# Decoder layer on one core: causal masks in VectorE's maxima, one transpose for a pair's maxima, results by ScalarE and GpSimd

## The chip, the cores and the metric

One Trainium2 chip, one NeuronCore of it. The metric is the device time of one launch in microseconds (us): 2375.72 us, the median of 3 runs (2371.66 to 2376.65). PE is TensorE's matmul side and PEld its weight load, DVE is VectorE, ACT is ScalarE, POOL is GpSimd, SP is SyncE.

## What is computed

A decoder layer for 8 sequences of 512 rows and 256 columns: linear attention, then the block that the change touches, then eight experts. The touched block is self attention with a causal mask plus cross attention to 1024 context rows, 16 heads of 16 columns each:

```python
att = jnp.where(causal[None, None], jnp.einsum('bhqd,bhkd->bhqk', q, k) * scale, -jnp.inf)
y = jnp.einsum('bhqk,bhkd->bhqd', jax.nn.softmax(att, axis=-1), v)
attc = jnp.einsum('bhqd,bhkd->bhqk', qc, kc) * scale
y = y + jnp.einsum('bhqk,bhkd->bhqd', jax.nn.softmax(attc, axis=-1), vc)
return y.transpose(0, 2, 1, 3).reshape(x.shape[0], T, C) @ Wp + bp
```

## The kernel before

The eight sequences are eight passes of one loop, each written out by hand for every engine. The part of a pass that the change touches treats the 16 heads as 8 pairs (`PAIRS`); the two heads of a pair stand on partitions 0 to 63 and 64 to 127 of `hq` (queries) and `hk` (keys), 16 columns split into high and low parts. Each pair goes through four kinds of work.

**Maxima.** The softmax needs each query row's largest score. A pair has 22 units (`MAXES`), 11 for each head. `max_unit` (L684) multiplies 128 queries with up to 512 keys into one of three PSUM banks, and `reduce` (L1297) takes the maximum over the columns into `craw`. 16 units are cross scores (L702, reduced at L1308, 512 columns each). The last 6 are self scores (L696, reduced at L1305): widths 512, then 384 and 128 together, then 256, each for both heads, so 8 matmuls and 8 reductions. The causal mask of their last 128 columns is added by TensorE itself, two bf16 matmuls of 128 columns for each (L698, `iden2` times `mqk2`, high and low rows of the partition half).

**The row.** After the last unit VectorE puts the maxima into `mpad` with two small operations (L1316, L1317). TensorE turns `mpad` with four 128 x 128 transposes (`maxima_rows`, L711), one for each block of 128 queries, and ScalarE copies the bank to `mrow` in one piece (L1112). Rows of `mrow`, times -1 in `minus`, are later subtracted from the scores by matmuls (L733, L739).

**Weights.** A pair has 11 units (`NU`): 3 of self and 8 of cross scores. `exp_scores` computes the transposed scores and subtracts the maxima in PSUM (`eslot`, two of them), ScalarE takes the exponential (L1118) into `es` (four of them, `ERING`), POOL zeroes what lies above the diagonal in the self units (L612), and `weigh` (L767) multiplies with the values, whose 17th column is 1 and gives the sum of the weights.

**Results.** After a pair's last `weigh`, ScalarE copies the sums to `zk` (L1127), `turn_results` (L771) transposes them into the next free one of the same three banks (L778), and VectorE's `results` (L1319) takes the reciprocals of the weight sums (L1324), multiplies (L1325), and adds self and cross parts into `y_s` (L1329). It waits for each step by a semaphore.

The order of all this is one list, `ORDER`, that `heads_order` writes and that every engine follows. In a repeated group of two weight units stand: two maxima units, the turn of an earlier pair if one is due, two `weigh`, two maxima units, two `exp_scores`. The maxima units belong to the pair after the one whose weights are taken (`AHEAD`), and the row follows four units after its last maximum (`ROW_AFTER`), for the last pair at once. The maxima, rows and turns share the ring of three banks: entry n may be written when entry n - 3 has been read (`ring_slot`, L673), and what reads it is VectorE for a maximum and a turn, ScalarE for a row:

```python
                    if kind == "row":
                        pe.wait_ge(s_mrow, cur(b, PAIRS, p + 1))
                    else:
                        pe.wait_ge(s_red, cur(b, NRED, RED_AT[former]))
```

Pair 0's maxima run before this, between feature products of the next pass (`FIRST_PARTS`); pairs 1 to 7 have theirs beside the weights of pairs 0 to 6; pair 7's weights have no maxima beside them. As a pair has 11 weight units and a group two, the turn falls alternately ahead of a pair's first self maxima and between the first and second two of them.

Of the kernel before, what the change touches and what calls it, by code (L numbers as in the profile page):

```python
# [21 lines left out]
P = 128  # L22
# [16 lines left out]
NEG = -1e30  # L39
HROW = 4 * XD  # L40
ZW = 32
# [56 lines left out]
BEHIND = 4  # L98

# [61 lines left out]

RING = [e for e in ORDER if e[0] in ("max", "row", "turn")]
RING_AT = {e: n for n, e in enumerate(RING)}
NRING, NRED = len(RING), sum(e[0] != "row" for e in RING)
RED_AT = {e: sum(f[0] != "row" for f in RING[:n + 1]) for n, e in enumerate(RING)}
# [39 lines left out]
def attentions(nc, x, xT, ctxT, wqkT, wv_l, rf, w_out, b_out, wk, bk, wq, bq, wv, bv, wck, bck,  # L205
# [9 lines left out]
    with ctx:  # L215
# [11 lines left out]
        mpad = sb("mpad", [P, NT, P])  # L227
# [19 lines left out]
        iden2 = sb("iden2", [P, 2, P], BF16)  # L247
        mqk2 = sb("mqk2", [P, 2, P], BF16)
# [40 lines left out]
        cstage = r_s[:, 0:3, :].rearrange("p n (s c) -> p n s c", s=2)  # L289
# [9 lines left out]
        minus = sb("minus", [P, 2], F32R)  # L299
        zk = sb("zk", [P, 2, T // 2])  # L300
# [76 lines left out]
        s_keep = sem("s_keep")  # L377
        s_ys = sem("s_ys")
        s_pace = sem("s_pace")
        s_blank = sem("s_blank")  # L380
        s_sent = sem("s_sent")
        s_route = sem("s_route")
        s_eid = sem("s_eid")

# [6 lines left out]
        LOADS = 42  # L391
# [7 lines left out]
        def _(sp):  # L399
# [29 lines left out]
            for n, src in enumerate((ident_d, mask_qk, mask_kq)):  # L429
                for half in range(2):  # L430
                    for at in range(2):
                        const(cstage[at * HROW:(at + 1) * HROW, n, half, :], src[half * HROW:(half + 1) * HROW])
# [120 lines left out]
            sp.wait_ge(s_av, NEXP * (nb + 1))  # L553
            for e in range(E):
                sp.dma_start(w2s[:, e * NHC * C:(e + 1) * NHC * C].rearrange("p (k c) -> p k c", k=NHC),
                             w2T[e].rearrange("(k p) c -> p k c", p=P)).then_inc(s_w2, 16)
# [9 lines left out]
        def _(pool):  # L566
# [14 lines left out]
            with pool.Fori(0, nb) as b:  # L581
# [23 lines left out]
                for p in range(PAIRS):  # L605
                    for n in range(NSELF):
                        k = p * NU + n
                        pool.wait_ge(s_exp, cur(b, NEXP, k + 1))
                        pool.sem_inc(s_past, 1)
                        for j, col in EXP_SELF[n]:  # L610
                            block = es[:, k % ERING, :].rearrange("p (a c) -> p a c", a=HB)[:, :, col:col + P]
                            last = nc.gpsimd.affine_select(block, block, [[0, HB], [1, P]], ALU.is_ge, 0.0, base=0,  # L612
                                                           channel_multiplier=-1)
                        last.then_inc(s_cut, 1)
# [13 lines left out]
        def _(pe):  # L628
# [44 lines left out]
            def ring_slot(b, entry):  # L673

                n = RING_AT[entry]
                if n >= MBANKS:
                    kind, p, _ = former = RING[n - MBANKS]
                    if kind == "row":
                        pe.wait_ge(s_mrow, cur(b, PAIRS, p + 1))
                    else:  # L680
                        pe.wait_ge(s_red, cur(b, NRED, RED_AT[former]))
                return mbank[n % MBANKS]

            def max_unit(b, p, m):  # L684
# [8 lines left out]
                if n >= 2 * NT:  # L693
                    for t, col in MAX_SELF[n - 2 * NT]:
                        w = (t + 1) * P
                        mm(pb[:, col:col + w], hq[i][at, t * P:(t + 1) * P], hk[i][at, 0:w], start=True, stop=False)  # L696
                        for half in range(2):
                            last = mm(pb[:, col + w - P:col + w], iden2[at, half, :], mqk2[at, half, :],  # L698
                                      start=False, stop=half == 1)
# [6 lines left out]
            def maxima_rows(b, p):  # L706
# [328 lines left out]
        def _(act):  # L1035
            act.sem_inc(s_mrow, PAIRS)
            act.sem_inc(s_exp, NEXP)
            act.sem_inc(s_keep, PAIRS)

# [11 lines left out]
            with act.Fori(0, nb) as b:  # L1051
# [54 lines left out]
                def maxima_rows(p):  # L1106
# [5 lines left out]
                    nc.scalar.activation(mrow[p % 2][:], mbank[n % MBANKS], ACT.Copy).then_inc(s_mrow, 1)  # L1112
# [15 lines left out]

                for kind, p, n in ORDER:
                    if kind == "row":  # L1130
                        maxima_rows(p)
# [582 lines left out]
```

## Time and profile before

| | us |
|---|---|
| median of 3 runs | 2375.72 |
| profiled execution, its own time | 2378.1 |
| its span | 2376.3 |
| PE busy | 2275.0 |
| DVE busy | 1400.3 |
| ACT busy | 1048.2 |
| POOL busy | 309.8 |

The busy time of a matmul reaches from its start to a modelled end, and neighbours overlap, so a share near 100% doesn't say that PE could take no more. In the timelines each line is one or several like instructions in a row; the bracket gives how long the engine stood idle before, and what ended that.

### The profile page before, as it was taken

The numbers are of one execution on the slowest core, as the hardware profiler recorded it, in microseconds if no ns is written. First come the engines' busy times: TensorE is split into PE (matmuls) and PEld (weight loads), VectorE is DVE, ScalarE is ACT, GpSimd is POOL, SyncE is SP. The second block draws the span as 40 slices with busy tenths as digits, with TensorE's granted clock in tenths as the row PEclk, the third lists the DMA queues.
The fourth block names the chain that finished last, engine by engine and source line by source line (L and its number), as shares of the span: only waits on it lengthen the run. The fifth ranks groups of instructions, "written<-read, shape, count | busy, mean of one in ns | idle before, by whom it ended". The sixth has DMA issues, their size and how long they took to land. (4 is left out here: it accounts for less than half of the span.)

```text
span 2376.3 us, 52163 instructions
## 1 busy us (share of the span) xinstructions
PE 2275.0 (96%) x17506; PEld 1439.5 (61%) x17507; DVE 1400.3 (59%) x3568; ACT 1048.2 (44%) x1432; POOL 309.8 (13%) x516
## 2 busy tenths in 40 slices
PE   8999999999999999999999999999999999799998
PEld 4556565656465556555565656564655565399997
DVE  2488347844685458734883478446854587244554
ACT  1256524652366226632564246513662266333332
POOL 1100011001110111011001111011101110122222
PEclk9989998999899989999899989998999999899999
DMA  7530034102520162006200441025201620555553
GB/s 231 202 105 24 2 131 163 46 2 81 191 68 2 47 225 68 2 11 226 81 24 2 150 144 46 2 81 191 68 2 43 229 68 2 179 182 179 178 185 113
DMA packets 115433, 236.19 MB, mean 99 GB/s; under 512 B 18638, under 2 KB 42319, under 8 KB 113008
## 3 DMA queue, kind: packets, MB, share of 16 engines
q1 hardware_dynamic: 111776, 224.55, 27.8%
q0 software_dynamic: 3408, 8.41, 1.0%
q8 instruction: 145, 2.38, 0.4%
q14 instruction: 104, 0.85, 0.1%
HBM read 160.66 MB, written 73.17 MB: 98 GB/s over the span
## 5 line engine op out<-in xcount | busy, mean ns | idle before, releaser
L1118 ACT ACTIVATE es<-ps 128x1024 f32<-128x1024 f32 (+1 forms) x704 | 659.9, 983 | 336.8 <-PE ps L739 252.6
L1308 DVE TENSOR_REDUCE craw<-ps 128x1 f32<-128x512 f32 x1024 | 641.1, 684 | 192.2 <-PE ps L702 180.5
L702 PE MATMUL ps<-hk,hq 64*128 64x512 f32 x1024 | 302.0, 497 | 20.0 <-DMA hq<-scr_qc 15.0
L767 PE MATMUL ps<-es,vca 128*17 128x256 f32 x4096 | 276.7, 382 | 1.2
L702 PEld LDWEIGHTS ps<-hk,hq 64*128 64x128 f32 x1024 | 143.1, 197 | 189.2 <-DVE craw L1308 109.8
L1305 DVE TENSOR_REDUCE craw<-ps 128x1 f32<-128x512 f32 (+3 forms) x512 | 218.7, 484 | 53.6 <-PE ps L698 49.8
L737 PE MATMUL ps<-hq,hk 64*128 64x512 f32 x1024 | 238.1, 429 | 1.5 <-ACT es L1118 1.5
L612 POOL TENSOR_SCALAR_AFFINE_SELECT es<-es 128x256 f32<-128x256 f32 x256 | 99.4, 407 | 1045.9 <-ACT es L1118 1045.9
L739 PE MATMUL ps<-mrow,minus 64*128 64x512 f32 x1024 | 219.1, 394 | 0.0
L1619 ACT ACTIVATE hT<-ph,b1s 128x128 f32<-128x128 f32 x312 | 89.2, 369 | 183.9 <-PE ph L1582 183.9
L767 PEld LDWEIGHTS ps<-es,vca 128*17 128x17 f32 x4096 | 93.8, 96 | 115.0 <-issue 62.4
L1582 PEld LDWEIGHTS ph<-xinT,w1s 128*128 128x128 f32 x1248 | 148.3, 195 | 3.1 <-issue 1.1
L1582 PE MATMUL ph<-xinT,w1s 128*128 128x128 f32 x1248 | 148.6, 278 | 0.7 <-ACT xinT L1609 0.7
L1595 PE MATMUL py<-w2s,hT 128*128 x624 | 141.1, 379 | 0.0
L787 PE MATMUL ps<-xT_s,wqf 128*128 128x512 f32 x288 | 138.5, 607 | 1.6 <-DVE wkf L1187 1.6
L737 PEld LDWEIGHTS ps<-hq,hk 64*128 64x128 f32 x1024 | 110.7, 186 | 40.8 <-ACT es L1118 23.3
L696 PE MATMUL ps<-hk,hq 64*128 64x512 f32 (+3 forms) x512 | 130.0, 388 | 4.6 <-DVE craw L1308 3.4
L797 PE MATMUL ps<-wkf,xT_s 128*128 128x512 f32 x288 | 130.3, 597 | 0.0
L1595 PEld LDWEIGHTS py<-w2s,hT 128*128 128x128 f32 x624 | 115.5, 190 | 14.1
L739 PEld LDWEIGHTS ps<-mrow,minus 64*128 64x128 f32 x1024 | 116.0, 187 | 9.9
L824 PE MATMUL ps<-big_b,x_s 128*128 128x512 f32 x256 | 118.2, 615 | 0.9 <-DVEq L1213 0.7
L1324 DVE RECIPROCAL rec<-ps 128x16 f32<-128x16 f32 x64 | 16.0, 250 | 172.1 <-PE ps L778 172.1
(206 smaller groups left out, 2883.6 us busy)
## 6 DMA issues: line engine op xcount, KB each, us to landing
w1s<-in_w1T SPq DMA_DIRECT2D x39, 1024.0 KB, 5.4
hk<-scr_kc SPq DMA_DIRECT2D x64, 512.0 KB, 5.4
scr_kc<-staged SPq DMA_DIRECT2D x16, 1024.0 KB, 4.7
scr_qc<-staged SPq DMA_DIRECT2D x32, 512.0 KB, 4.9
scr_q<-staged SPq DMA_DIRECT2D x32, 512.0 KB, 5.5
hq<-scr_qc SPq DMA_DIRECT2D x64, 256.0 KB, 5.0
hq<-scr_q SPq DMA_DIRECT2D x64, 256.0 KB, 4.2
hk<-scr_k SPq DMA_DIRECT2D x64, 256.0 KB, 5.1
```

Source lines behind the costliest of these rows:

```text
L696: mm(pb[:, col:col + w], hq[i][at, t * P:(t + 1) * P], hk[i][at, 0:w], start=True, stop=False)
L702: last = mm(pb, hq[i][at, T + t * P:T + (t + 1) * P], hk[i][at, T + half * BANK:T + (half + 1) * BANK], start=True, stop=True)
L737: mm(pb[a], hk[i][at, T + j * P:T + (j + 1) * P], hq[i][at, T:2 * T], start=True, stop=False)
L739: last = mm(pb[a], neg[a], mrow[p % 2][at, :], start=False, stop=True)
L767: last = mm(z[row:row + VW, (2 - len(tiles)) * P:2 * P], (va if own else vca)[:, j, p * HB + a, :], weights, start=n in (0, NSELF), stop=n ...
L787: last = mm(t[:, a * T:(a + 1) * T], wqf[:, c, j * P:(j + 1) * P], xT_s[:, c, :], start=c == 0, stop=c == KC - 1)
L797: last = mm(t[:, half * 512:(half + 1) * 512], xT_s[:, c, i * P:(i + 1) * P], wkf[:, c, half * 512:(half + 1) * 512], start=c == 0, stop=c ...
L1118: nc.scalar.activation(es[:, k % ERING, :].rearrange("p (a c) -> p a c", a=HB)[:, :, 0:w], eslot[k % 2][:].rearrange("p (a c) -> p a c", a ...
L1305: last = v.reduce_max(craw[p % 2][:, t, a:a + 1, 2], pb[:, col:col + (t + 1) * P], AX.X)
L1308: last = v.reduce_max(craw[p % 2][:, t, a:a + 1, half], pb, AX.X)
L1582: last = mm(ph[g % 2][:, a * TILE:(a + 1) * TILE], w1s[i][:, k, (GROUP * c + a) * P:(GROUP * c + a + 1) * P], xinT[i][:, k, :], start=k == ...
L1595: last = mm(py[i][:, n, 0:C], hT[i][:, c, n * P:(n + 1) * P], w2s[:, bass.ds(e * (NHC * C) + c * C, C)], start=c == 0, stop=c == NHC - 1)
```

## The change

- The self maxima lose their mask matmuls (L698). VectorE adds the mask instead: one `tensor_tensor_reduce` reads the scores in PSUM, adds `causal` (bf16, 384 zeros and then the triangle of mask values, of which the last columns are taken), writes the sum back over the scores and gives the maximum.
- The maxima of all four query blocks go into one 128 x 128 `mpad`, 16 columns for each head and block, by one operation. One transpose turns it. ScalarE fills `mrow` with four copies of the same 128 columns, each scaled for each partition by `inblock` (1 where the partition belongs to that block, else 0). `minus` has -1 in the two rows of each block.
- A turned result is copied by ScalarE to `zt` in SBUF (`turned`), VectorE takes only the reciprocals from it, and POOL multiplies and adds. This holds for pairs 0 to 6; the last pair stays with VectorE. VectorE's reciprocals stand two maxima units later in its own order (`DVE_ORDER`, `LATER`). The bank of a turn is free when ScalarE has copied it.
- At the start, 11 small loads of constants are gone and the masks' tiles are built otherwise. `sp` waits once more before the loads of the experts' weights.

```diff
@@ order and ring @@
+def reciprocals_later():
+    order = [e for e in ORDER if e[0] in ("max", "turn")]
+    for p in range(PAIRS - 1):
+        at = order.index(("turn", p, 0))
+        order.insert(min(at + 1 + LATER, order.index(("turn", p + 1, 0))), order[at])
+        del order[at]
+    return order
...
                     if kind == "row":
                         pe.wait_ge(s_mrow, cur(b, PAIRS, p + 1))
+                    elif kind == "turn" and former != LAST_TURN:
+                        pe.wait_ge(s_zt, cur(b, PAIRS - 1, p + 1))
                     else:
                         pe.wait_ge(s_red, cur(b, NRED, RED_AT[former]))
@@ TensorE @@
                     for t, col in MAX_SELF[n - 2 * NT]:
                         w = (t + 1) * P
-                        mm(pb[:, col:col + w], hq[i][at, t * P:(t + 1) * P], hk[i][at, 0:w], start=True, stop=False)
-                        for half in range(2):
-                            last = mm(pb[:, col + w - P:col + w], iden2[at, half, :], mqk2[at, half, :],
-                                      start=False, stop=half == 1)
+                        last = mm(pb[:, col:col + w], hq[i][at, t * P:(t + 1) * P], hk[i][at, 0:w], start=True, stop=True)
...
-                for t in range(NT):
-                    last = tr(pb[:, t * P:(t + 1) * P], mpad[:, t, :], ident[:])
-                last.then_inc(s_ring, 1)
+                tr(pb[:, 0:P], mpad[:], ident[:]).then_inc(s_ring, 1)
@@ ScalarE @@
-                    nc.scalar.activation(mrow[p % 2][:], mbank[n % MBANKS], ACT.Copy).then_inc(s_mrow, 1)
+                    for t in range(NT):
+                        last = nc.scalar.activation(mrow[p % 2][:, t * P:(t + 1) * P], mbank[n % MBANKS][:, 0:P],
+                                                    ACT.Copy, scale=inblock[:, t:t + 1])
+                    last.then_inc(s_mrow, 1)
...
+                def turned(p):
+                    s = RING_AT["turn", p, 0]
+                    act.wait_ge(s_ring, cur(b, NRING, s + 1))
+                    act.wait_ge(s_ys, cur(b, PAIRS, p))
+                    tv = mbank[s % MBANKS].rearrange("p (n d) -> p n d", d=ZW)
+                    nc.scalar.activation(zt[:], tv[:, :, 0:VW], ACT.Copy).then_inc(s_zt, 1)
@@ GpSimd @@
+                def results(p):
+                    pool.wait_ge(s_rec, b * (PAIRS - 1) + (p + 1))
+                    pool.sem_inc(s_past, 1)
+                    nc.gpsimd.tensor_tensor(yn[:], zt[:, :, 0:XD], rec[:].unsqueeze(2).broadcast_to([P, 2 * NT * HB, XD]),
+                                            ALU.mult).then_inc(s_yn, 1)
+                    pool.wait_ge(s_yn, b * (PAIRS - 1) + (p + 1))
+                    pool.sem_inc(s_past, 1)
+                    rows = sums_of()
+                    nc.gpsimd.tensor_tensor(y_s[:, :, p * HB * XD:(p + 1) * HB * XD], rows[:, 0], rows[:, 1],
+                                            ALU.add).then_inc(s_ys, 1)
@@ VectorE @@
                     if n >= 2 * NT:
+                        dve.sem_inc(s_held, 1)
                         for t, col in MAX_SELF[n - 2 * NT]:
-                            last = v.reduce_max(craw[p % 2][:, t, a:a + 1, 2], pb[:, col:col + (t + 1) * P], AX.X)
+                            own = pb[:, col:col + (t + 1) * P]
+                            last = v.tensor_tensor_reduce(own, own, causal[:, (NT - 1 - t) * P:NT * P], 1.0, LOWEST,
+                                                          ALU.add, ALU.max, craw[p % 2][:, t, a:a + 1, 0])
...
-                        raw = [craw[p % 2][:, :, :, w] for w in range(3)]
-                        rows = mpad[:].rearrange("p t (a c) -> p t a c", a=HB)
-                        v.tensor_copy(rows[:, :, :, 0], raw[2])
-                        v.tensor_tensor(rows[:, :, :, 1], raw[0], raw[1], ALU.max).then_inc(s_max, 1)
+                        rows = mpad[:].rearrange("p (a t c) -> p t a c", a=HB, t=NT)
+                        v.tensor_tensor(rows[:, :, :, 0:2], craw[p % 2][:, :, :, 0:2], craw[p % 2][:, :, :, 0:3:2],
+                                        ALU.max).then_inc(s_max, 1)
...
+                def reciprocals(p):
+                    dve.wait_ge(s_zt, cur(b, PAIRS - 1, p + 1))
+                    v.reciprocal(rec[:], zt[:, :, XD]).then_inc(s_rec, 1)
```

VectorE, at the turn that falls ahead of a pair's self maxima, before (from the last cross maximum of the pair to the end of the results; REGISTER_ALU rows are waits):

```order
L1308 TENSOR_REDUCE craw<-ps 128x1
L1322 REGISTER_ALU
L1324 RECIPROCAL rec<-ps 128x16
L1228 REGISTER_ALU
L1325 TENSOR_TENSOR yn<-ps,rec 128x256
L1327 REGISTER_ALU
L1329 TENSOR_TENSOR y_s<-yn 128x4x32
```

and the same place with the change:

```order
L1365 TENSOR_REDUCE craw<-ps 128x1
L1355 REGISTER_ALU
L1361 ISA ps,craw<-ps,causal 128x512
L1361 ISA craw 128x1
L1355 REGISTER_ALU
L1361 ISA ps,craw<-ps,causal 128x512
L1361 ISA craw 128x1
L1377 REGISTER_ALU
L1378 RECIPROCAL rec<-zt 128x16
L1355 REGISTER_ALU
L1361 ISA ps,craw<-ps,causal 128x384
L1361 ISA craw 128x1
```

Two of VectorE's three operations on the results are gone, and the third stands between the self maxima. Each masked maximum is two instructions, the second of which writes `craw` alone.

ScalarE, from the copy of a turned result to the copy of the next pair's maxima, with the change:

```order
L1177 ISA
L1179 ACTIVATE zt<-ps 128x272
L1160 REGISTER_ALU
L1162 ACTIVATE es<-ps 128x1024
L1160 REGISTER_ALU
L1162 ACTIVATE es<-ps 128x1024
L1160 REGISTER_ALU
L1162 ACTIVATE es<-ps 128x1024
L1160 REGISTER_ALU
L1162 ACTIVATE es<-ps 128x1024
L1150 REGISTER_ALU
L1154 ACTIVATE mrow<-ps,inblock 128x128 x4
```

The copy to `zt` (L1179) is new and stands behind the two exponentials of its group; the copies to `mrow` were one of 128 x 512.

## Rows read from the trace of the kernel before

**Rows 1.** The page, part 1: busy time of TensorE, its share of the span, instructions.
```profile
PE 2275.0 (96%) x17506; PEld 1439.5 (61%) x17507; DVE 1400.3 (59%) x3568; ACT 1048.2 (44%) x1432; POOL 309.8 (13%) x516
```
**Rows 2.** Window of two pairs: length, then PE, PEld, DVE, ACT, POOL busy, clock, DMA share.
```profile
441.80:475.90 34.10, 33.79 (x377) 20.65 (x374) 28.85 (x59) 22.67 (x27) 2.79 (x8) 1.00 0.03 11
```
**Rows 3.** Timeline, one steady group: start, length, engine, line, operation, [idle before].
```profile
167.65 1.06 PE L767 MATMUL ps<-es,vca 128*17 128x256 f32 x16
...
169.17 3.98 DVE L1308 TENSOR_REDUCE craw<-ps 128x1 f32<-128x512 f32 x6 [0.21 <-PE ps L702]
...
170.34 1.06 PE L767 MATMUL ps<-es,vca 128*17 128x256 f32 x16
```
**Rows 4.** Timeline, a pair whose turn falls ahead of its self maxima.
```profile
173.21 0.66 PE L778 MATMUL ps<-ident,zk 128*128 128x128 f32 x4
...
175.00 0.51 PE L696 MATMUL ps<-hk,hq 64*128 64x512 f32 x2
...
175.67 1.29 DVE L1305 TENSOR_REDUCE craw<-ps 128x1 f32<-128x512 f32 x2 [0.36 <-PE ps L698]
...
176.45 0.33 PE L696 MATMUL ps<-hk,hq 64*128 64x384 f32 x1
...
177.44 0.41 PE L767 MATMUL ps<-es,va 128*17 128x128 f32 x8
...
178.76 0.76 DVE L1305 TENSOR_REDUCE craw<-ps 128x1 f32<-128x256 f32 x2 [0.16 <-PE ps L698]
...
179.98 2.72 DVE L1308 TENSOR_REDUCE craw<-ps 128x1 f32<-128x512 f32 x4
...
181.40 0.65 PE L711 MATMUL ps<-ident,mpad 128*128 128x128 f32 x4
...
181.98 0.50 PE L737 MATMUL ps<-hq,hk 64*128 64x512 f32 x2
182.09 0.60 ACT L1112 ACTIVATE mrow<-ps 128x512 fp32r<-128x512 f32 x1 [0.85 <-PE ps L711]
```
**Rows 5.** Timeline, a pair whose turn falls between its self maxima.
```profile
157.62 1.29 DVE L1305 TENSOR_REDUCE craw<-ps 128x1 f32<-128x512 f32 x2 [0.84 <-PE ps L698]
...
159.10 0.44 PE L696 MATMUL ps<-hk,hq 64*128 64x384 f32 x1
...
159.97 2.12 DVE L1305 TENSOR_REDUCE craw<-ps 128x1 f32<-128x384 f32 x6
...
162.42 0.50 PE L702 MATMUL ps<-hk,hq 64*128 64x512 f32 x2
...
162.95 2.48 DVE L1308 TENSOR_REDUCE craw<-ps 128x1 f32<-128x512 f32 x4 [0.49 <-PE ps L702]
...
163.68 0.51 PE L702 MATMUL ps<-hk,hq 64*128 64x512 f32 x2
```
**Rows 6.** Timeline of the start: first use of the loaded constants by VectorE and TensorE.
```profile
38.51 0.30 DVE L1191 CAST iden<-r_s 128x256 bf16<-128x256 f32 x1 [20.65 <-DMA gb_bc<-in_gate_b]
...
45.54 1.03 PE L813 MATMUL ps<-wp_s,bv_c 128*128 128x256 f32 x4
```
**Rows 7.** Timeline: pair 0's eight self reductions at a stretch.
```profile
377.23 3.27 DVE L1305 TENSOR_REDUCE craw<-ps 128x1 f32<-128x512 f32 x8
```
**Rows 8.** VectorE: a sum from PSUM by group, and two small operations of the timeline.
```profile
L1272 DVE TENSOR_TENSOR r_s<-ps,xb 128x512 f32<-128x512 f32 x32 | 22.1, 692 | 145.6 <-PE ps L912 103.6 <-PE ps L965 41.9
...
280.87 0.17 DVE L1406 TENSOR_SCALAR mv<-mv 128x4 f32<-128x4 f32 x1
280.94 0.16 DVE L1407 TENSOR_SCALAR mv<-mv 128x4 f32<-128x4 f32 x1
```
**Rows 9.** Groups of the page: a ScalarE operation with a per-partition operand.
```profile
L1619 ACT ACTIVATE hT<-ph,b1s 128x128 f32<-128x128 f32 x312 | 89.2, 369 | 183.9 <-PE ph L1582 183.9
```
**Rows 10.** POOL: a product-sized sum by group, and the wait before a pair's cuts.
```profile
L1523 POOL TENSOR_TENSOR base<-xin,b2s 128x256 f32<-128x256 f32 x39 | 28.8, 740 | 14.4 <-issue 13.6
...
187.44 0.41 POOL L612 TENSOR_SCALAR_AFFINE_SELECT es<-es 128x256 f32<-128x256 f32 x1 [14.16 <-ACT es L1118]
```

More of the change, by code:

```diff
@@ L39 @@
 NEG = -1e30
+LOWEST = -3.0e38
 HROW = 4 * XD
+MROW = HROW // NT
 ZW = 32
@@ L98 @@
 BEHIND = 4
+LATER = 2
 SWAP = (0, 1)
@@ L160 @@
 ORDER = heads_order()
+def reciprocals_later():
[5 more added lines that the diff above has]
+    return order
+DVE_ORDER = reciprocals_later()
 RING = [e for e in ORDER if e[0] in ("max", "row", "turn")]
 RING_AT = {e: n for n, e in enumerate(RING)}
-NRING, NRED = len(RING), sum(e[0] != "row" for e in RING)
-RED_AT = {e: sum(f[0] != "row" for f in RING[:n + 1]) for n, e in enumerate(RING)}
+NRING, NRED = len(RING), sum(e[0] == "max" for e in RING) + 1
+LAST_TURN = ("turn", PAIRS - 1, 0)
+RED_AT = {e: sum(f[0] == "max" or f == LAST_TURN for f in RING[:n + 1]) for n, e in enumerate(RING)}
 NEXP = PAIRS * NU
@@ L226, in attentions @@
         mrow = [sb(f"mrow{i}", [P, T], F32R) for i in range(2)]
-        mpad = sb("mpad", [P, NT, P])
+        mpad = sb("mpad", [P, P])
+        zt = sb("zt", [P, 2 * NT * HB, VW])
+        sb("spare", [P, (NT - 1) * P - 2 * NT * HB * VW])
         wq_s = sb("wq_s", [P, KC, C])
@@ L390, in attentions @@
         WJ = NPAIR // 2
-        LOADS = 42
+        LOADS = 31
         SEL_DMA = 4 * NQ
@@ L428, in _ @@
             const(number[:], number_d)
-            for n, src in enumerate((ident_d, mask_qk, mask_kq)):
-                for half in range(2):
-                    for at in range(2):
-                        const(cstage[at * HROW:(at + 1) * HROW, n, half, :], src[half * HROW:(half + 1) * HROW])
+            const(r_s[:, 0, 0:P], mask_qk)
             const(wvl[:], wv_l.rearrange("(k p) r -> p k r", p=P))
@@ L1131, in _ @@
                         maxima_rows(p)
+                    elif kind == "turn" and p < PAIRS - 1:
+                        turned(p)
                     elif kind == "exp":
@@ L1197, in _ @@
                             iota[:, 0:E].unsqueeze(1).broadcast_to([P, E + 1, E]), ALU.is_gt)
-            for a in range(HB):
-                at = slice(a * HROW, (a + 1) * HROW)
-                v.tensor_scalar(minus[at], ident[at, a * HROW:a * HROW + 2], -1.0, None, ALU.mult)
+            v.reduce_sum(minus_f[:], ident[:].rearrange("p (b c) -> p c b", c=MROW)[:, 0:2, :], AX.X)
+            v.reduce_sum(inblock[:], ident[:].rearrange("p (a t c) -> p t a c", a=HB, t=NT), AX.XY)
             v.tensor_tensor(bv_c[:, 0, :], bv_c[:, 0, :], bv_c[:, 1, :], ALU.add).then_inc(s_fold, 1)
@@ L1327, in results @@
                     dve.wait_ge(s_red, cur(b, NRED, RED_AT["turn", p, 0]))
-                    rows = yn[:].rearrange("p (w t a) d -> p w t (a d)", w=2, t=NT)
+                    rows = sums_of()
                     v.tensor_tensor(y_s[:, :, p * HB * XD:(p + 1) * HB * XD], rows[:, 0], rows[:, 1], ALU.add).then_inc(s_ys, 1)
                     dve.wait_ge(s_ys, cur(b, PAIRS, p + 1))
-                for kind, p, n in ORDER:
+                for kind, p, n in DVE_ORDER:
                     if kind == "max":
                         reduce(p, n)
+                    elif kind == "turn" and p == PAIRS - 1:
+                        last_results()
                     elif kind == "turn":
-                        results(p)
+                        reciprocals(p)
                 dve.wait_ge(s_xb, cur(b, 2, 2))
```

52 lines of the change are left out of this document (33 added, 19 removed).

## The prediction

> **What bounds the kernel now.** I read the page first. TensorE is busy 96% of the span and VectorE 59% [rows 1], which would make this a TensorE kernel in which VectorE costs nothing. But the average covers three different stages, and a matmul's busy time reaches to a modelled end. So I went on to a window of two pairs inside the touched stage: 34.10 us, or 17.05 us a pair, of which VectorE is busy 28.85 us, 85% [rows 2]. ScalarE has 22.67 us and POOL 2.79 us. Both TensorE and VectorE are near their limit there, and which one waits has to be read from the timeline.
>
> In a steady group TensorE's `weigh` returns every 2.69 us (167.65 to 170.34), while VectorE stands idle 0.21 us before it goes on [rows 3]. TensorE sets the pace and VectorE follows with a tenth to spare. Around the self maxima this differs from pair to pair. With the turn ahead of them, TensorE issues the turn at 173.21 and the first self maximum only at 175.00. VectorE fills that hole with the results and is still idle 0.36 us before it reduces at 175.67 [rows 4]. With the turn between them, the results stand in VectorE's way: the next self maximum is issued at 159.10, its reduction starts at 159.97 [rows 5].
>
> **The change, part by part.** In a pass 7 pairs have their maxima beside weights. I count 3 with the turn ahead, 3 with it between, and 1 without a turn.
>
> *TensorE, masks.* From the first self maxima to the next maxima it takes 175.00 to 176.45, 1.45 us [rows 4]; the same step with unmasked maxima takes 162.42 to 163.68, 1.26 us [rows 5]. So four mask matmuls cost 0.19 us, and a pair's sixteen 0.76 us.
>
> *TensorE, the row.* Four transposes hold it from 181.40 to 181.98, 0.58 us [rows 4]; three fewer save 0.43 us. Together TensorE sheds 1.19 us a pair, and no pair can gain more.
>
> *VectorE, masked maxima.* The eight self reductions of a pair take 3.27 us in a row [rows 7]. Each becomes a sum with a maximum plus a second instruction that writes the maximum. Let x be what one costs above the reduction it replaces. No row shows the new operation, so I bound it. A sum of 512 columns from PSUM takes 0.692 us [rows 8]; two reductions of that size take 1.29 us together [rows 4], 0.645 each with their overlap. So the sum itself adds 0 to 0.05. The second instruction is small: two small operations without a wait between them start 0.07 us apart (280.87, 280.94), and one lasts 0.17 us [rows 8]. That gives x = 0.07 at the least and 0.22 if nothing overlaps. I don't exclude less than 0.07 by rows, but a second instruction can't be free. I take 0.11, nearer the lower end: the pair has no semaphore between its halves.
>
> The Trainium skill ("VectorE: DVE Perf Modes", section "Two Vector instructions with no wait between them") says that an operation which also writes out its accumulator is two instructions, and that the second is judged on its own for being held. By that the read-out would not be held here, all operands starting at partition 0, and the sum would go by the lower end. No run here shows it.
>
> *VectorE, results and row.* The product and the sum leave; the reciprocals stay at no more than 0.25 us, and as they now read SBUF I take 0.20. Of the two operations for `mpad` one goes, 0.08 us: the step from the last reduction's end (178.76 + 0.76 = 179.52) to the next (179.98) shrinks from 0.46 to 0.38 [rows 4].
>
> *Turn ahead.* From first self reduction to first cross reduction it is now 179.98 - 175.67 = 4.31 us [rows 4]. After: it begins 0.19 earlier (no masks) and lasts 3.27 + 8x + 0.20 + 0.38. VectorE reaches the next pair 0.65 - 8x earlier. The results that left had been in a hole, and the reciprocals move from the hole into the busy stretch. The row's transposes wait for the maxima that VectorE takes next, and with their 0.43 TensorE gains 1.08 - 8x.
>
> *Turn between.* Now 162.95 - 157.62 = 5.33 us [rows 5]. The maximum at 159.10 comes 0.19 earlier, its reduction can start 0.48 behind it (175.67 - 175.00 less 0.19), at 159.39. Then 2.12 + 6x + 0.20 + 0.38 reaches 162.09 + 6x instead of 162.95. With the row: 1.29 - 6x.
>
> *No turn.* As the first, without reciprocals: 1.28 - 8x.
>
> *ScalarE.* `mrow` takes four operations with a per-partition operand; such ones take 89.2 / 312 = 0.286 us each [rows 9], so 1.14 us instead of 0.60. ScalarE stood idle 0.85 us before it [rows 4] and the row comes earlier, so most is covered; between 0 and the full 0.54 I take 0.1, since the exponentials behind it have two buffers. The copy to `zt` is shorter than 0.60 us and finds an engine that is a third idle [rows 2]. Behind it stand the next exponentials; if they come late, TensorE's `exp_scores` is next to wait.
>
> *POOL.* Two operations of at most 0.74 us each [rows 10], while the next pair's cuts are awaited for 14.16 us. They cost nothing; without this cover they would delay the cuts, and `weigh` behind them, by 1.5 us a pair. They release `zt` long before the next turn.
>
> *Pair 0.* There the eight reductions stand in a row [rows 7] and TensorE waits. They get 8x - 0.08 longer, and TensorE gets 0.43 back: a loss of 8x - 0.51.
>
> *The start.* VectorE has the constants at 38.51 and TensorE needs them at 45.54 [rows 6]. Eleven loads fewer make them earlier, which nobody waits for. Semaphore bookkeeping and the last pair are costed at nothing; their work lies behind TensorE's features.
>
> *Sum per pass:* 3 (1.08 - 8x) + 3 (1.29 - 6x) + (1.28 - 8x) - 0.7 for ScalarE - (8x - 0.51) = 8.20 - 58x us. With x = 0.11 that is 1.82 us, times 8 passes 15 us. The profiled execution's own time is 2378.1 us, 2.4 above the median, so it would give 2363, and the median goes from 2375.7 to **2361 us**. The sum is zero at x = 0.141. With x = 0.07 it is 33 us, 2343; with 0.22 it is -36 us, 2412.
>
> **Rivals.**
>
> *VectorE becomes the bound, slower.* Place: the self maxima of every pair. If the second instruction runs without overlap (x = 0.20), the loss is 3.4 us a pass, 27 us in all: 2403. It decides from x = 0.141. For it: VectorE is at 85% already, and in the stretch with the turn ahead it loses its hole. Against: small operations without waits do overlap. Chance 0.25.
>
> *The masked maximum runs at half rate.* It reads a bank and writes the same one. Each of the eight would last another 3.27 / 8 = 0.41 us, x = 0.52: 8.20 - 30.2 = -22.0 us a pass, 2552. The sum from PSUM at 0.692 speaks against it. The Trainium skill ("Vector Engine (DVE) Microarchitecture Reference", section "Points that are easy to get wrong") has a rule near it, that an accumulating operation of the scalar-tensor-tensor shape runs at half throughput with two non-bf16 sources in SBUF; here one source is in PSUM and the other bf16, so its condition isn't met. Chance 0.05.
>
> *Nothing measurable.* x between 0.131 and 0.151 leaves less than 5 us, the 0.2% that a measurement of this kernel can tell from no change: 2376. Chance 0.13.
>
> *TensorE gains all it sheds.* 1.19 us for 7 pairs and 8 passes is 67 us: 2309. It needs x near 0, against the second instruction that the program shows. Chance 0.05; the forecast has 0.52.
>
> **The numbers.** Faster by over 0.2%: forecast and full gain, 0.57. Within: 0.13. Slower: 0.30. The range reaches down to x = 0.07 with ScalarE costing nothing (8.20 + 0.7 - 4.06 = 4.84 us a pass, 39 us: 2337) and up to x = 0.20, 2403.
>
> **What would show it.** Right: the masks' matmuls gone, the `weigh` period of 2.69 us unchanged, a self stretch (first masked maximum to first cross reduction) of 4.7 us with the turn ahead, eight masked maxima some 0.9 us above 3.27, VectorE's idle time before the self maxima about 1 us with the turn ahead, a pair near 16.8 us instead of 17.05. Wrong: second instructions 0.15 us apart or more from the next, TensorE waiting for the masked maxima between self units, or exponentials starting late behind `mrow`.

## The result and the profile after

| | before | after |
|---|---|---|
| median, us | 2374.26 (4 runs) | 2342.89 (4 runs) |
| profiled execution: span, us | 2376.3 | 2340.5 |

The ratio is 0.9863, 95% interval 0.9843 to 0.9884: 28 to 37 us faster, 31 by the medians and 35.8 by the two spans. Forecast were 15 us and 2361; the direction was right, the size half of what came.

Part 1 of the page of the kernel after, beside [rows 1]:

```profile
PE 2231.4 (95%) x16290; PEld 1402.7 (60%) x16291; DVE 1369.7 (59%) x3905; ACT 1098.8 (47%) x1680; POOL 368.3 (16%) x628
```

TensorE has 1216 instructions fewer: 1024 mask matmuls and 192 transposes. VectorE is busy 31 us less although it has 337 instructions more, 512 of them read-outs. The groups of the new operations (us busy, mean ns of one | us idle before, and what ended that):

```profile
L1361 DVE CUSTOM_DVE_ANT_0 ps<-ps,causal 128x512 f32<-128x512 f32 (+3 forms) x512 | 235.5, 517 | 78.8 <-PE ps L741 78.8
L1154 ACT ACTIVATE mrow<-ps,inblock 128x128 fp32r<-128x128 f32 x256 | 73.4, 375 | 80.5 <-PE ps L752 80.5
L645 POOL TENSOR_TENSOR yn<-zt,rec 128x256 f32<-128x256 f32 x56 | 34.9, 622 | 253.8 <-DVE rec L1378 253.8
L650 POOL TENSOR_TENSOR y_s<-yn 128x128 f32<-128x128 f32 x56 | 25.7, 459 | 10.0 <-POOL yn L645 10.0
L1179 ACT ACTIVATE zt<-ps 128x272 f32<-128x272 f32 x56 | 22.2, 397 | 8.6 <-PE ps L818 8.6
L1378 DVE RECIPROCAL rec<-zt 128x16 f32<-128x16 f32 x56 | 13.9, 248 | 104.3 <-ACT zt L1179 104.3
```

The timeline after, of a pair whose turn falls ahead of its self maxima, as [rows 4]:

```profile
171.56 0.66 PE L818 MATMUL ps<-ident,zk 128*128 128x128 f32 x4
...
173.36 0.50 PE L741 MATMUL ps<-hk,hq 64*128 64x512 f32 x2
...
174.04 0.70 DVE L1361 CUSTOM_DVE_ANT_0 ps<-ps,causal 128x512 f32<-128x512 f32 x1 [1.34 <-PE ps L741]
...
174.66 0.14 DVE L1361 DVE_READ_ACCUMULATOR2_ANT craw<- 128x1 f32 x1
174.66 0.73 DVE L1361 CUSTOM_DVE_ANT_0 ps<-ps,causal 128x512 f32<-128x512 f32 x1
...
178.08 2.68 DVE L1365 TENSOR_REDUCE craw<-ps 128x1 f32<-128x512 f32 x4
...
179.50 0.32 PE L752 MATMUL ps<-ident,mpad 128*128 128x128 f32 x1
...
179.86 1.14 ACT L1154 ACTIVATE mrow<-ps,inblock 128x128 fp32r<-128x128 f32 x4 [0.67 <-PE ps L752]
...
181.24 1.06 PE L807 MATMUL ps<-es,vca 128*17 128x256 f32 x16
```

From the first self reduction to the first cross reduction it is now 178.08 - 174.04 = 4.04 us, where it was 4.31. The prediction had named 4.7 us for this stretch as a sign of being right, and about 1 us for VectorE's idle time ahead of it, which is 1.34. The line to look at is the read-out, the second instruction of a masked maximum: it starts at 174.66, the very moment at which the next masked maximum starts. From one masked maximum of 512 columns to the next it is 0.62 us.

The same for a pair whose turn falls between its self maxima, as [rows 5], down to the same `weigh` four pairs later:

```profile
155.62 0.63 PE L807 MATMUL ps<-es,va 128*17 128x256 f32 x8
...
158.19 0.58 PE L741 MATMUL ps<-hk,hq 64*128 64x384 f32 x3
...
158.88 0.57 DVE L1361 CUSTOM_DVE_ANT_0 ps<-ps,causal 128x384 f32<-128x384 f32 x1 [0.61 <-PE ps L741]
...
161.65 2.48 DVE L1365 TENSOR_REDUCE craw<-ps 128x1 f32<-128x512 f32 x4
...
163.06 0.32 PE L752 MATMUL ps<-ident,mpad 128*128 128x128 f32 x1 [0.17 <-DVE craw L1365]
...
221.84 0.63 PE L807 MATMUL ps<-es,va 128*17 128x256 f32 x8
```

and of the kernel before, the same stretch with its results, its transposes and the `weigh` behind them:

```profile
156.40 0.63 PE L767 MATMUL ps<-es,va 128*17 128x256 f32 x8
...
159.56 0.29 DVE L1329 TENSOR_TENSOR y_s<-yn 128x128 f32<-128x128 f32 x1
...
164.37 0.65 PE L711 MATMUL ps<-ident,mpad 128*128 128x128 f32 x4 [0.18 <-DVE craw L1308]
164.95 1.06 PE L767 MATMUL ps<-es,vca 128*17 128x256 f32 x16
...
225.28 0.63 PE L767 MATMUL ps<-es,va 128*17 128x256 f32 x8
```

From the first `weigh` row to the last, four pairs, it is 68.88 us before and 66.22 after. This **four-pair period** is free of the start, the end and the noise of whole runs (the second pass gives 68.87 and 66.24), so it is taken from every kernel below. Counted from one pair later it is 68.87 and 66.23; where a kernel's period depends on the pair from which it is counted, that is said.

### The profile page after: what moved, and what is told of

Same layout as the page of the kernel before. It is cut to its first block and busy times, and to the rows that moved or that the text cites. A ratio compares the mean times of both kernels' runs of the same rounds, so it can differ in the third digit from the quotient of the medians.

```text
span 2340.5 us, 50923 instructions
## 1 busy us (share of the span) xinstructions
PE 2231.4 (95%) x16290; PEld 1402.7 (60%) x16291; DVE 1369.7 (59%) x3905; ACT 1098.8 (47%) x1680; POOL 368.3 (16%) x628
## 5 line engine op out<-in xcount | busy, mean ns | idle before, releaser
L744 PE MATMUL ps<-hk,hq 64*128 64x512 f32 x1024 | 310.1, 503 | 20.2 <-DMA hq<-scr_qc 14.8
L1361 DVE CUSTOM_DVE_ANT_0 ps<-ps,causal 128x512 f32<-128x512 f32 (+3 forms) x512 | 235.5, 517 | 78.8 <-PE ps L741 78.8
L744 PEld LDWEIGHTS ps<-hk,hq 64*128 64x128 f32 x1024 | 153.5, 197 | 190.4 <-DVE craw L1365 118.7
L741 PE MATMUL ps<-hk,hq 64*128 64x512 f32 (+3 forms) x512 | 124.6, 373 | 10.1 <-DVE craw L1361 5.1
L952 PE MATMUL ps<-big_c,big_a 128*128 128x256 f32 x512 | 112.6, 381 | 2.8 <-ACT big_c L1122 2.8
```

The source lines that it names most:

```text
L741: last = mm(pb[:, col:col + w], hq[i][at, t * P:(t + 1) * P], hk[i][at, 0:w], start=True, stop=True)
L744: last = mm(pb, hq[i][at, T + t * P:T + (t + 1) * P], hk[i][at, T + half * BANK:T + (half + 1) * BANK], start=True, stop=True)
L1361: last = v.tensor_tensor_reduce(own, own, causal[:, (NT - 1 - t) * P:NT * P], 1.0, LOWEST, ALU.add, ALU.max, craw[p % 2][:, t, a:a + 1, 0])
```

## Experiments

Three readings stood against each other: two engines share the bound, by the forecast's formula (A); TensorE alone bounds (B); VectorE alone bounds (C). Each run undoes a part of the change, or does one alone. The cuts of code show the lines that matter most.

**Masks by TensorE again**, with VectorE's plain maxima, the rest as changed:

```diff
-                        last = mm(pb[:, col:col + w], hq[i][at, t * P:(t + 1) * P], hk[i][at, 0:w], start=True, stop=True)
+                        mm(pb[:, col:col + w], hq[i][at, t * P:(t + 1) * P], hk[i][at, 0:w], start=True, stop=False)
+                        for half in range(2):
+                            last = mm(pb[:, col + w - P:col + w], iden2[at, half, :], mqk2[at, half, :],
+                                      start=False, stop=half == 1)
```

> The changed kernel with the masks back on TensorE (two bf16 matmuls each, as before) and plain maxima on VectorE; the single transpose and the results' new owners stay. Changed kernel: 2343 us. Theory A (the two engines share the bound: what TensorE sheds in masks VectorE gets in return, 0.76 us against 0.4 us a pair, and half the stretches are limited by each): some 1 us a pass is lost, about 2350. Theory B (TensorE alone is the bound): all 0.76 us of 8 pairs and 8 passes are lost, 49 us, about 2392. Theory C (VectorE alone is the bound): 0.4 us a pair is won, 24 us, about 2319.

Measured: 2355.06 us, ratio 0.9911 (0.9888 to 0.9934), period 67.93. Slower by 12 us, where A said some 7, B 49, and C said faster: nearest to A. The masks gain where they are, on VectorE.

**Four transposes again**, of the one `mpad`, with the four scaled copies kept:

```diff
-                tr(pb[:, 0:P], mpad[:], ident[:]).then_inc(s_ring, 1)
+                for t in range(NT):
+                    last = tr(pb[:, t * P:(t + 1) * P], mpad[:], ident[:])
+                last.then_inc(s_ring, 1)
```

> The changed kernel, but the one transpose of the row is issued four times, to the four quarters of the bank (only the first is read). This adds TensorE's 0.43 us a pair and nothing else. Theory A and theory B: 0.43 us for 8 pairs and 8 passes, 27 us slower, about 2370. Theory C: the row's transposes lie beside VectorE's work, no more than 5 us slower.

Measured: 2363.53, ratio 0.9948 (0.9933 to 0.9963), period 67.30. 20.6 us slower, where A and B said 27 and C at most 5. The three transposes are worth 1.08 us in four pairs, less than the 1.72 (4 times 0.43) forecast.

**Results by VectorE again**, at the old place in its order:

```diff
-                    elif kind == "turn" and p == PAIRS - 1:
-                        last_results()
                     elif kind == "turn":
-                        reciprocals(p)
+                        last_results(p)
```

> The changed kernel with the results as before: VectorE takes reciprocals, product and sum from the bank right at the turn, ScalarE and POOL have no part in them. Theory A: VectorE has a hole where the turn falls ahead of the self maxima, and is in the way only where it falls between them: 0.8 us lost in 3 pairs, 0.16 us won in 3, 1.9 us a pass, 15 us slower, about 2358. Theory C: 0.87 us in 6 pairs and 8 passes, 42 us slower, about 2385. Theory B: the same as the changed kernel, 2343.

Measured: 2356.5, ratio 0.9921 (0.9898 to 0.9944), period 67.55, or 67.18 counted from one pair later. By the time this is A's 2358; what the loss is made of is another matter (below, at the masks alone).

**Maxima without the mask.** Plain reductions over the same columns, masked ones included; so the mask is left out of the maxima, and the weights above the diagonal are still zeroed by POOL:

```diff
-                            last = v.tensor_tensor_reduce(own, own, causal[:, (NT - 1 - t) * P:NT * P], 1.0, LOWEST,
-                                                          ALU.add, ALU.max, craw[p % 2][:, t, a:a + 1, 0])
+                            last = v.reduce_max(craw[p % 2][:, t, a:a + 1, 0], pb[:, col:col + (t + 1) * P], AX.X)
```

> The changed kernel with plain maxima over the unmasked self scores: the mask is left out of the maxima (not out of the weights, where GpSimd's cuts stay), so a row subtracts a larger number than it needs, which cancels in the softmax. It takes the masked maximum's extra cost x away and gives x by the trace. Theory A: 0.38 us of VectorE a pair are on the path wherever it is late: 2.6 us a pass, 21 us faster, about 2322. Theory B: no change, 2343. Theory C: 24 us faster, about 2319.

Measured: 2327.12, ratio 0.9795 (0.9773 to 0.9818), period 64.91, which beats both kernels. It lies nearer to A (2322) and C (2319) than to B (2343); C was excluded by the first run. A maximum over more columns is still an upper bound, and the softmax divides it out again, as long as no masked score stands so far above a row's others that their exponentials vanish. Its timeline at the place of 174.04 above:

```profile
173.89 0.50 PE L741 MATMUL ps<-hk,hq 64*128 64x512 f32 x2
...
174.43 1.29 DVE L1359 TENSOR_REDUCE craw<-ps 128x1 f32<-128x512 f32 x2 [1.19 <-PE ps L741]
...
175.79 2.01 DVE L1359 TENSOR_REDUCE craw<-ps 128x1 f32<-128x384 f32 x6
...
178.07 1.29 DVE L1362 TENSOR_REDUCE craw<-ps 128x1 f32<-128x512 f32 x2
```

This prices the operation directly: 178.07 - 174.43 = 3.64 us against 4.04, so 0.40 for eight, **x = 0.05 us**. The periods say the same: 66.22 - 64.91 = 1.31 for 32, 0.04 each.

The rows show a second price that x doesn't hold. A plain maximum starts 0.54 us after its scores are issued (173.89 to 174.43), a masked one 0.68 (173.36 to 174.04), and the first pass has 0.53 to 0.54 and 0.68 to 0.69 wherever VectorE waits for self scores. Whether the operation makes these 0.14 or the semaphore increment that stands ahead of it (`s_held`, gone in this run too) was not tried.

Beside the first run this one prices the mask matmuls alone, as VectorE works alike in both: 67.93 - 64.91 = 3.02 us for 64, **0.76 us a pair**, all of what the forecast said TensorE would shed. The masked maxima take 1.31 of it back, and 1.71 is left, 0.43 a pair.

**The reciprocals at once** (`LATER = 0` instead of 2), with the masked and with the unmasked maxima:

> The changed kernel with LATER = 0: VectorE takes the reciprocals right behind the turn in its order instead of two maxima units later. Changed kernel: 2343. Theory A: 0.16 us of reciprocals leave the busy stretch for the hole ahead of or between the self maxima, in 6 pairs of 8 passes, 8 us, about 2335. The rival: ScalarE's copy to zt comes too late behind its exponentials, VectorE waits for it, and the maxima behind it with it; 0.3 us in 6 pairs would be 14 us slower, about 2357.

> The unmasked maxima (the mask left out of the maxima alone, as in the run before) with LATER = 0. Unmasked alone: 2327. Theory A: another 8 us, about 2319. If TensorE is the bound once VectorE has the masks off: 2327.

Measured: 2339.85, ratio 0.9842 (0.9818 to 0.9866), period 66.08; and 2326.23, ratio 0.9776 (0.9751 to 0.9801). The intervals overlap those of the kernels with 2. A's 8 us aren't seen in either, nor the rival's loss; the second came out at the 2327 expected if TensorE bounds once the masks are off VectorE. The periods of the second are 64.72 and, counted from one pair later, 64.68 where it was 64.90; of the first, 66.08 and 66.46, 0.14 less and 0.23 more. So where the reciprocals stand is worth some 0.2 us in four pairs, with the masked maxima in either direction; it isn't settled whether anything in the whole run.

**One part alone, with the row half undone.** Masks alone, then results alone, each with four transposes and the four scaled copies (the edits are those above, combined):

> Of the change only the masks in VectorE's maxima: the results are VectorE's as before, and the row has four transposes (ScalarE's four copies stay). Kernel before: 2376. Theory A with x = 0.05: with the turn ahead of the self maxima the results lie in a hole and 0.37 us is won; with the turn between them the results stay in the way and 0.1 is won; less 0.4 for pair 0: 1.4 us a pass, 11 us, about 2365. Theory B: 0.76 us for 8 pairs and 8 passes, 49 us, about 2327. Theory C: VectorE has 0.4 us more a pair, 24 us slower, about 2400.

> Of the change only the results' new owners (ScalarE copies, VectorE takes reciprocals two units later, POOL multiplies and adds): masks on TensorE as before, four transposes (ScalarE's four copies and the single operation for mpad stay). Kernel before: 2376. Theory A: with masks on TensorE the hole is there in any case; 0.27 less 0.16 us is won in 3 pairs, 3 us, about 2372. Theory C: 0.87 us in 6 pairs and 8 passes, 42 us, about 2334. Theory B: 2376.

Measured: 2372.84, ratio 0.9978 (0.9966 to 0.9991), period 68.62; and 2381.16, ratio 1.0014 (1.0005 to 1.0024), period 69.04. All three readings miss: A by 8 and 9 us, B by 46 and 5, C by 27 and 47. Either ScalarE's copies cost what the parts gain, or the parts gain next to nothing alone. The last four runs separate these. "Old row" is the row as before, save that one operation still fills `mpad`:

```diff
-        mpad = sb("mpad", [P, P])
+        mpad = sb("mpad", [P, NT, P])
...
-                tr(pb[:, 0:P], mpad[:], ident[:]).then_inc(s_ring, 1)
+                for t in range(NT):
+                    last = tr(pb[:, t * P:(t + 1) * P], mpad[:, t, :], ident[:])
+                last.then_inc(s_ring, 1)
...
-                    for t in range(NT):
-                        last = nc.scalar.activation(mrow[p % 2][:, t * P:(t + 1) * P], mbank[n % MBANKS][:, 0:P],
-                                                    ACT.Copy, scale=inblock[:, t:t + 1])
-                    last.then_inc(s_mrow, 1)
+                    nc.scalar.activation(mrow[p % 2][:], mbank[n % MBANKS], ACT.Copy).then_inc(s_mrow, 1)
```

> The kernel before (masks by TensorE, results by VectorE) with the new row alone: one mpad, one transpose, four scaled copies. Additive: the row was worth 20.6 us between the full change and the one with four transposes, 26.3 us between masks on TensorE with and without it; so 2377 less 20 to 26, about 2354, two thirds of the whole gain by itself. Interplay (the row needs VectorE's lighter load to pay): under 12 us, 2366 or more.

> Masks by VectorE alone, with the row as before throughout: four blocks of mpad, four transposes, one copy of 512 columns by ScalarE. Beside the run with four transposes and four copies (2372.8) this takes only ScalarE's three extra copies away. If the copies cost what the forecast gave them, 0.7 us a pass: 2367. If they are hidden: 2373. If they cost their full 0.54 us for each of 7 pairs, 30 us: 2343.

> Results by ScalarE and GpSimd alone, with the row as before throughout. Beside the run with four transposes and four copies (2381.2) this takes only the three extra copies away. Copies at 0.7 us a pass: 2375.5, nothing gained by the results themselves. Copies hidden: 2381. Moving the results pays by itself (VectorE alone bounds): under 2370.

> The whole change except the row: masks by VectorE, results moved, but four blocks of mpad, four transposes and one copy. Beside the run with four transposes and four copies (2363.5): copies at 0.7 us a pass give 2358, hidden copies 2363. With this and the first run of this job the row as a whole (fewer transposes, more copies) is priced on both backgrounds: additive if before less the row alone and this less the whole change are the same within 4 us, about 18 us by the first price.

Measured: 2355.27, 2373.74, 2375.32 and 2361.56 us, before 2375.14 on the same chip. The row is additive, as expected: before less the row alone is 19.9 us, the change with the old row less the whole change 18.7 (these two on different chips). Of the copies, the masks' run says hidden, the results' run says 0.7 us a pass, the last lies between; the periods decide it (below).

All the combinations of the three parts (the ratios are each to the runs of before on its own chip):

| masks by VectorE | results moved | new row | median, us | ratio (95%) | four-pair period, us |
|---|---|---|---|---|---|
| | | | 2374.26 | 1 | 68.88 |
| yes | | | 2373.74 | 0.9998 (0.9984 to 1.0012) | 68.60 |
| | yes | | 2375.32 | 0.9995 (0.9979 to 1.0011) | 69.03 |
| | | yes | 2355.27 | 0.9916 (0.9892 to 0.9941) | 67.96 |
| yes | yes | | 2361.56 | 0.9933 (0.9907 to 0.9958) | 67.29 |
| | yes | yes | 2355.06 | 0.9911 (0.9888 to 0.9934) | 67.93 |
| yes | | yes | 2356.50 | 0.9921 (0.9898 to 0.9944) | 67.55 |
| yes | yes | yes | 2342.89 | 0.9863 (0.9843 to 0.9884) | 66.22 |

By the periods the masks alone gain 0.28 us in four pairs and the results alone lose 0.15. Counted from one pair later the masks alone gain more, 68.87 - 68.23 = 0.64: wherever the masked maxima stand with VectorE's own results 0.37 us are lost at one place in a pass, which is read below. The runs' ratios, 0.9978 and 0.9998 for the masks, 1.0014 and 0.9995 for the results, are a few us either way. Both together gain 1.59 (1.56 from one pair later). The row adds 0.92 by itself and 1.05 to 1.10 beside the others: its worth hardly depends on them. And ScalarE's three extra copies are free: without and with them the period is 68.60 and 68.62, 69.03 and 69.04, 67.29 and 67.30.

**Why the masks gain next to nothing alone.** Timeline of the kernel with the masks alone and the old row, turn between:

```profile
156.57 0.63 PE L799 MATMUL ps<-es,va 128*17 128x256 f32 x8
...
159.14 0.58 PE L731 MATMUL ps<-hk,hq 64*128 64x384 f32 x3
...
159.82 0.29 DVE L1376 TENSOR_TENSOR y_s<-yn 128x128 f32<-128x128 f32 x1
...
160.76 0.57 DVE L1347 CUSTOM_DVE_ANT_0 ps<-ps,causal 128x384 f32<-128x384 f32 x1 [0.64 <-DVE y_s L1376]
...
161.69 0.38 PE L731 MATMUL ps<-hk,hq 64*128 64x256 f32 x1 [0.93 <-DVE craw L1347]
...
164.94 0.65 PE L743 MATMUL ps<-ident,mpad 128*128 128x128 f32 x4 [0.17 <-DVE craw L1351]
...
173.78 0.66 PE L810 MATMUL ps<-ident,zk 128*128 128x128 f32 x4
...
181.61 0.65 PE L743 MATMUL ps<-ident,mpad 128*128 128x128 f32 x4
```

TensorE issues the scores at 159.14 and VectorE takes them only at 160.76, 1.62 us later, where it takes 0.69 in the kernel after (158.19 to 158.88). The results stand between until 159.82 + 0.29 = 160.11, and another 0.64 us pass behind them; TensorE then waits 0.93 us for a bank. From the `weigh` to the transposes it takes 8.37 us, before 164.37 - 156.40 = 7.97: 0.40 lost. In the later turns of this kind in the pass VectorE goes on sooner after its results (0.27 us instead of the 0.64 in the row), and the stretch is 8.03 and 8.00. So nothing of the shed mask matmuls arrives there. With the turn ahead, from the turn to the transposes, it is 181.61 - 173.78 = 7.83 against 8.19 [rows 4], 0.36 won.

The kernel after needs 7.44, 7.42 and 7.44 us at the three places with the turn between: 0.93, 0.61 and 0.56 less. Less the gap of 0.64 or 0.27 each time this leaves 0.3. So by this estimate, in which a gap counts in full, the gap behind the results is two thirds of what moving them gives at the first place and nearly half at the others, and the operations' own time is the rest; the forecast and A had only the operations. With the turn ahead moving them costs 0.11, 7.83 to 7.94: two such places and the first two of the others make 0.93 + 0.61 - 0.22 = 1.32 us, and the periods 68.60 - 67.29 = 1.31.

TensorE's waits for the masked maxima show it over the whole run (first row: us in total, times, longest). The second row has VectorE's own gaps behind its results, in this kernel:

```profile
PE ps L731 <- DVE craw L1347: 21.8, 46, 0.9
...
DVE ps L1347 <- DVE y_s L1376: 9.5, 24, 0.6
```

with the results moved too, in the kernel after, the first is a quarter and the second is gone:

```profile
PE ps L741 <- DVE craw L1361: 5.1, 21, 0.4
```

**Why the results gain nothing alone.** The same place with the results alone and the old row:

```profile
158.59 0.63 PE L816 MATMUL ps<-es,va 128*17 128x256 f32 x8
...
161.29 0.44 PE L745 MATMUL ps<-hk,hq 64*128 64x384 f32 x1
...
162.14 1.42 DVE L1365 TENSOR_REDUCE craw<-ps 128x1 f32<-128x384 f32 x4 [1.04 <-PE ps L747]
...
166.56 0.65 PE L760 MATMUL ps<-ident,mpad 128*128 128x128 f32 x4 [0.17 <-DVE craw L1368]
```

The place of the results is now 1.04 us of idle time, ended by TensorE's mask matmuls. The reduction follows the issue of its maximum by 0.85 us; before it was 159.97 - 159.10 = 0.87, with the results in between. And 166.56 - 158.59 = 7.97, as before. With the masks on TensorE the results were not in the way there; the later places of this kind take 7.97 in both kernels too.

**What the row is worth.** Transposes and the next `weigh` with the turn ahead, in the kernel with the row alone:

```profile
178.46 2.72 DVE L1359 TENSOR_REDUCE craw<-ps 128x1 f32<-128x512 f32 x4 [0.16 <-PE ps L744]
...
179.88 0.32 PE L752 MATMUL ps<-ident,mpad 128*128 128x128 f32 x1
...
180.94 0.47 PEld L744 LDWEIGHTS ps<-hk,hq 64*128 64x128 f32 x2
...
181.66 1.06 PE L807 MATMUL ps<-es,vca 128*17 128x256 f32 x16
```

and in the kernel before, behind the transposes at 181.40 [rows 4]:

```profile
182.79 0.19 PEld L702 LDWEIGHTS ps<-hk,hq 64*128 64x128 f32 x2
...
183.34 1.06 PE L767 MATMUL ps<-es,vca 128*17 128x256 f32 x16
```

The transpose holds TensorE some 0.26 us now (163.06 to the `weigh` at 163.32 in the kernel after) instead of 0.58, 0.32 less. But with the turn ahead only 0.16 arrives: from the transposes to `weigh` it was 1.94 us and is 1.78. The two maxima between them go up to VectorE's bank: their loads take 0.47 instead of 0.19, and VectorE, whose reductions must free that bank, ends the four at 178.46 + 2.72 = 181.18. With the turn between, all 0.32 arrives: from the first `weigh` to the one behind the transposes it was 164.95 - 156.40 = 8.55 and is 8.23 in this kernel. Two pairs of each kind make 0.96, the period's 0.92.

## Why the prediction was right in direction and half in size

**x, the term that failed.** The formula was 8.20 - 58x us a pass with x = 0.11 and 0.07 as the lower bound. x is 0.05. This is the step of the prediction that failed: "a second instruction can't be free". I priced it by the distance of two small operations, 0.07 us [rows 8]. The trace after shows the next main operation starting together with the read-out, so the read-out takes no place of its own. Of the 0.40 us that are left for eight, most lies in the sums being a little longer than the reductions: 714, 574, 451 and 329 ns on average for the four widths, where the reductions take 686, 552, 419 and 280, which makes 0.26. The Trainium skill ("VectorE: DVE Perf Modes", section "Two Vector instructions with no wait between them") counts two instructions and lets the second be judged by itself; the trace has two records, and no gap stands before the read-outs, so it agrees. That sentence alone would have argued for the low end and below it. With x = 0.05 the formula gives 5.30 us a pass, 42 us. So x alone is 58 x 0.06 = 3.5 us a pass, 28 us of the run; the charge for ScalarE was 0.7 us a pass too high and the row's gain, by the periods, some 1.2 too high, and these two partly cancel.

**The stretches held in their sums, partly by luck.** The formula's parts without the row, at x = 0.05: turn ahead 0.65 - 8x = 0.25, measured 8.19 - (179.50 - 171.56) = 0.25; turn between 0.86 - 6x = 0.56, measured 7.97 - (163.06 - 155.62) = 0.53. Twice their sum, 1.56, is the four-pair period's 1.59 with the old row. But the terms inside didn't hold. With the turn ahead the first self reduction was to begin 0.19 earlier; it begins 174.04 - 171.56 = 2.48 us behind the turn, before 175.67 - 173.21 = 2.46. Without mask matmuls a plain maximum does start sooner behind its scores, 0.54 against 0.67, but a masked one gives 0.14 of it back. And the stretch to the first cross reduction was to last 3.85 + 8x = 4.25 and lasts 4.04: with plain maxima it lasts 3.64, 0.21 under the 3.85 (the reductions and the steps behind them each a little shorter). 0.21 lost and 0.21 won cancel, which nothing in the working foresaw. With the turn between, the start 0.48 behind the scores was in truth 0.69.

**The reading behind one of them did not.** "The results stand in VectorE's way" [rows 5] was wrong for the kernel before: removed alone, they left idle time. They come into the way only when the masks have left TensorE, and then by the gap behind them as much as by their own time. The forecast took both changes at once, so its number came out while its reason for [rows 5] did not. It is also why A missed both runs of one part: it added up gains of which most exist only together, and had no gap behind the results.

**The row** was sized 0.43 us a pair, three quarters of 0.58. One transpose alone costs 0.26, more than a quarter, and with the turn ahead half of the rest doesn't arrive: 0.32 and 0.16.

**ScalarE** was charged 0.7 us a pass for its copies. They last 1.14 us as forecast, but cost nothing: three pairs of kernels with equal periods. The sign that the prediction named for a cost, exponentials late behind `mrow`, is there with the turn ahead:

```profile
180.09 0.40 PE L779 MATMUL ps<-mrow,minus 64*128 64x512 f32 x2
...
180.87 1.96 ACT L1162 ACTIVATE es<-ps 128x1024 f32<-128x1024 f32 x2
...
183.23 1.94 ACT L1162 ACTIVATE es<-ps 128x1024 f32<-128x1024 f32 x2 [0.40 <-PE ps L779]
```

The exponentials start 0.78 us behind the matmuls that release them, where before it was 182.76 - 182.32 = 0.44. But the next ones wait 0.40 us for TensorE again, so the delay is swallowed.

**POOL, the constants, the semaphores** were put at nothing. POOL's two operations take 0.62 and 0.46 us, and outside POOL the waits for it are the same before and after (TensorE's weight loads, 2.9 us for the `es` that it cuts). No run changes the constants alone. For the semaphores it isn't shown: an increment stands ahead of the masked maxima, which start 0.14 us late.

**Pair 0** was to lose 8x - 0.51, which at the measured x is a gain of 0.11. TensorE's wait for `mpad` there, first before, then after:

```profile
PE ps L711 <- DVE mpad L1317: 9.7, 8, 1.2
```

```profile
PE ps L752 <- DVE mpad L1372: 11.6, 8, 1.4
```

It grew by 0.24 us a pass, against 0.32 from the transposes.

**The sum with measured terms:** seven pairs at 2.66 / 4 us are 4.66 us a pass, pair 0 gives 0.08; 4.7 us times 8 are 38, beside 35.8 by the spans and 31 (28 to 37) by the runs. The remainder wasn't traced.

**The rivals.** VectorE as the bound, slower: its mechanism is seen where the results stay with VectorE, and even there it only cancels the gain. Half rate: a masked maximum of 512 columns takes 0.714 us against 0.686 for a reduction, so no; this is in line with the Trainium skill ("Vector Engine (DVE) Microarchitecture Reference", section "Points that are easy to get wrong"), whose rule asks for two sources in SBUF that are not bf16; this case doesn't test the rule. Full gain for TensorE: 67 us, not reached even without masks (49 by the ratio of that run), since the row gives 0.32 at most where 0.43 was counted and half of that with the turn ahead; the mask matmuls' 0.76 a pair did arrive.

## What to carry to other kernels

When two engines are both near their limit, price an edit together with the one that unloads the other: work moved from the first to the second and work moved off the second were worth 0.3 to 0.6 us and -0.15 us in 69 alone, and 1.6 together, so a test of each by itself would hardly have kept either. Test "this work is in the way" by asking what starts after it and what that waited for last; an engine that goes on 0.1 us behind its own work may still have had to wait for another. Check the terms of a formula as well as its total: here two of them were each 0.21 us off and the total was right. And ask what a step needs rather than what it had: maxima that serve only as a bound need no mask.

## What the runs showed of the hardware

- A masked maximum starts 0.68 to 0.69 us after its scores are issued, a plain reduction 0.53 to 0.54 (where VectorE waits for self scores in the first pass; the kernel after and the unmasked one). The semaphore increment ahead of it is a possible cause that was not separated.
- The read-out of a masked maximum (0.14 us) starts with the next masked maximum and adds no distance between them: 0.62 us from one of 512 columns to the next (174.04 to 174.66).
- After VectorE's own sum into `y_s`, a plain reduction goes on 0.12 us behind its end (159.56 + 0.29 to 159.97 [rows 5]). A masked maximum goes on 0.64 us behind it at the first such turn of a pass and 0.27 at the two others (in the three passes read; 8 x 0.64 + 16 x 0.27 = 9.4 of the 9.5 us shown above), and its 0.37 us more are the difference between the stretches of 8.37 and 8.00. A semaphore increment of its own stands ahead of the masked maxima and not of the reductions; whether it or the operation makes the gap, and why two lengths, was not tried.
- Four ScalarE copies of 128 x 128 in a row, each with a scale for each partition, take 1.14 us, 0.375 each and overlapped, where one of 128 x 512 takes 0.60.
